# Attention on one core: the bank of a head's output sums changes place with a bank of the transposed scores at every new head

## The reference

```python
qkv = jnp.einsum('btd,de->bte', x, w_qkv) + b_qkv
q, k, v = heads(q), heads(k), heads(v)          # (4, 16, 2048, 16)
q, k = _rope(q), _rope(k)
attn = jnp.einsum('bhqd,bhkd->bhqk', q, k) / math.sqrt(HEAD_DIM)
attn = jax.nn.softmax(attn, axis=-1)
out = jnp.einsum('bhqk,bhkd->bhqd', attn, v)
x = _layernorm(x + out.reshape(b, t, d) @ w_out + b_out)      # shortened
x = _layernorm(x + (silu(x @ wg.T) * (x @ wu.T)) @ wd.T)      # shortened
```

## Time and profile before

| | |
|---|---|
| runs, device us | 2869.18, 2868.82, 2866.64 |
| span of the profiled execution | 2868.1 us |
| mean granted TensorE clock | 0.989 |
| PE matmul / DVE / ACT / POOL busy | 98% / 94% / 90% / 49% |
| copies of the sums (line 1032) | 64, the first at 274.6 us, the last at 2546.3 us |

### The profile page before, as it was taken

One profiled execution on the slowest core, in us unless ns is written; L12 is line 12 of the kernel. 1 busy time (PEld: TensorE's weight loads), 2 busy tenths in 40 slices (PEclk: granted clock), 3 DMA queues, 4 the chain that ended last, 5 costly groups with the idle time before them and its releaser, 6 DMA issues. The chain is left out here.

```text
span 2868.1 us, 70575 instructions
## 1 busy us (share of the span) xinstructions
PE 2811.7 (98%) x27022; PEld 862.5 (30%) x27022; DVE 2702.9 (94%) x3088; ACT 2591.9 (90%) x4778; POOL 1416.7 (49%) x4133
## 2 busy tenths in 40 slices
PE   8989999999999999999999999999999999999998
PEld 4531222222222222222222222222222222246665
DVE  7989999999999999999999999999999999947777
ACT  5756999999999999999999999999999999976555
POOL 7851444444444444444444444444444444436553
PEclk9978999999999999999999999999999999999999
DMA  5431111111111111111111111111111111233431
GB/s 194 142 116 28 36 35 36 35 36 35 35 35 35 34 35 36 35 36 36 35 35 35 36 35 35 35 35 36 35 35 36 35 35 35 70 90 92 118 96 38
DMA packets 121519, 146.56 MB, mean 51 GB/s; under 512 B 52832, under 2 KB 87520, under 8 KB 121180
## 3 DMA queue, kind: packets, MB, share of 16 engines
q1 hardware_dynamic: 120892, 142.02, 17.0%
q10 hardware_dynamic: 288, 0.01, 0.0%
HBM read 106.30 MB, written 35.13 MB: 49 GB/s over the span
## 5 line engine op out<-in xcount | busy, mean ns | idle before, releaser
L102 DVE TENSOR_REDUCE tile_max<-s_ps 128x1 f32<-128x1024 f32 (+1 forms) x2048 | 2282.4, 1185 | 8.8 <-PE s_ps L91 2.8
L1063 ACT ACTIVATE probs<-st_ps 128x512 f32<-128x512 f32 x4096 | 2202.2, 601 | 71.0 <-PE st_ps L942 41.1
L953 PE MATMUL o_ps<-probs,kept_v 128*17 128x256 f32 x16384 | 1283.1, 385 | 25.7 <-ACT sums L1032 25.7
L91 PE MATMUL s_ps<-k,q 64*128 64x512 f16 x4096 | 1266.2, 386 | 11.0 <-DVE tile_max L102 9.2
L942 PE MATMUL st_ps<-q,k 64*128 64x512 f16 x4096 | 1249.5, 382 | 1.1 <-ACT probs L1063 0.8
L1198 POOL TENSOR_TENSOR larger<-spared 128x256 f32<-128x256 f32 x1107 | 342.8, 310 | 675.6 <-ACT spared L1038 598.5
L953 PEld LDWEIGHTS o_ps<-probs,kept_v 128*17 128x17 f32 x16384 | 273.6, 95 | 852.2 <-ACT probs L1063 445.6
L942 PEld LDWEIGHTS st_ps<-q,k 64*128 64x128 f16 x4096 | 256.1, 94 | 902.0 <-ACT probs L1063 842.3
L1207 POOL TENSOR_TENSOR spared<-spared,larger 128x256 f32<-128x256 f32 x984 | 318.4, 324 | 81.9
L1200 POOL TENSOR_SCALAR larger<-larger 128x256 f32<-128x256 f32 x1107 | 261.4, 236 | 96.8
L91 PEld LDWEIGHTS s_ps<-k,q 64*128 64x128 f16 x4096 | 250.2, 94 | 50.4 <-DVE tile_max L102 46.5
(11 more groups left out here) (119 smaller groups left out, 1625.3 us busy)
## 6 DMA issues: line engine op xcount, KB each, us to landing
q<-q_parts SPq DMA_DIRECT2D x193, 128.0 KB
k<-k_parts SPq DMA_DIRECT2D x193, 128.0 KB
x_t<-in_x_t SPq DMA_DIRECT2D x16, 512.0 KB, 7.2
q_parts<-parts SPq DMA_DIRECT2D x32, 256.0 KB, 2.6
k_parts<-parts SPq DMA_DIRECT2D x32, 256.0 KB, 2.6
heads_out<-sums SPq DMA_DIRECT2D x256, 32.0 KB, 2.1
kept_v<-heads_out SPq DMA_DIRECT2D x16, 512.0 KB, 6.1
kept_v<-inverses_out SPq DMA_DIRECT2D x32, 256.0 KB
```

The source lines that it names most:

```text
L91: mm = pe.matmul(s["s_ps"][g % 2][:, j * BANK:(j + 1) * BANK], s["q"][h % 2][rows, r // KW * P:(r // KW + 1) * P], s["k"][h % 2][rows, at: ...
L102: dve.tensor_reduce(s["tile_max"][h % 2][:, r // KW, r % KW:r % KW + 1], s["s_ps"][g % 2][:, columns], AX.X, ALU.max).then_inc(s["s_read"], 1)
L953: mm = pe.matmul(o_ps[c * 32:c * 32 + VM, at:at + HALF], t["kept"][:, h, kt, :], probs[(h * KT + kt) % RING][:, c * BANK + at:c * BANK + a ...
L1063: act.activation(probs[(h * KT + kt) % RING][:, c * BANK:(c + 1) * BANK], st_ps[n % ST][:, :], ACT.Exp, scale=scale).then_inc(exp_done, 1)
```

## The change

There are four banks, `bank_ps0` to `bank_ps3`, and a table made before the program is written says which one each score and each head's sums use. Head 0 sums in bank 3, and its scores go round banks 0 to 2. The sums of every later head use the bank in which its own score 4 stood. That place in the ring would next be used by score 7 (4 + 3); score 7 and those after it in that place use the bank of the head before's sums instead.

The waits follow. The first sums of a head wait for one more exponential, that of score 4, and no longer for the copy of the head before. Score 7 waits for that copy, and no longer for the exponential of score 4 (which ScalarE does before the copy). Nothing else is added or taken away: the numbers of matmuls, exponentials and copies are the same.

```diff
+    HANDED = QC
+    ring = list(range(ST))
+    sum_bank, score_bank = [ST], []
+    for h in range(HEADS):
+        if h > 0:
+            sum_bank.append(ring[(h * EXPS + HANDED) % ST])
+        for e in range(EXPS):
+            if h > 0 and e == HANDED + ST:
+                ring[(h * EXPS + e) % ST] = sum_bank[h - 1]
+            score_bank.append(ring[(h * EXPS + e) % ST])
...
-        st_ps = [psum(f"st_ps{i}", [P, BANK]) for i in range(ST)]
-        o_ps = psum("o_ps", [P, BANK])
+        banks = [psum(f"bank_ps{i}", [P, BANK]) for i in range(ST + 1)]
+        st_ps = [banks[i] for i in score_bank]
+        o_ps = [banks[i] for i in sum_bank]
...
-                wait(pe, exp_done, n - ST + 1)
-                pe.matmul(st_ps[n % ST][:, :], k[h % 2][rows, kt * P:(kt + 1) * P],
+                if h > 0 and e == HANDED + ST:
+                    pe.wait_ge(sums_out, h)
+                else:
+                    wait(pe, exp_done, n - ST + 1)
+                pe.matmul(st_ps[n][:, :], k[h % 2][rows, kt * P:(kt + 1) * P],
                           q[h % 2][rows, c * BANK:(c + 1) * BANK], start=True, stop=True).then_inc(st_done, 1)
...
-                    pe.wait_ge(exp_done, h * EXPS + (kt + 1) * QC)
-                    if kt == 0:
-                        wait(pe, sums_out, h)
+                    handed = kt == 0 and h > 0
+                    pe.wait_ge(exp_done, h * EXPS + (HANDED + 1 if handed else (kt + 1) * QC))
...
-                    mm = pe.matmul(o_ps[c * 32:c * 32 + VM, at:at + HALF], t["kept"][:, h, kt, :],
+                    mm = pe.matmul(o_ps[h][c * 32:c * 32 + VM, at:at + HALF], t["kept"][:, h, kt, :],
...
-                act.copy(out["sums"][i][:, :], o_ps[:, :]).then_inc(sums_out, 1)
+                act.copy(out["sums"][i][:, :], o_ps[h][:, :]).then_inc(sums_out, 1)
```

More of the change, by code:

```diff
@@ L1062, in _ @@
                     act.wait_ge(st_done, n + 1)
-                    act.activation(probs[(h * KT + kt) % RING][:, c * BANK:(c + 1) * BANK], st_ps[n % ST][:, :],
+                    act.activation(probs[(h * KT + kt) % RING][:, c * BANK:(c + 1) * BANK], st_ps[n][:, :],
                                    ACT.Exp, scale=scale).then_inc(exp_done, 1)
-                    if e == QC and h > 0:
+                    if e == HANDED and h > 0:
                         drain(h - 1)
@@ L1077, in clear @@
             def clear():
-                dve.memset(o_ps[:, :], 0.0).then_inc(o_cleared, 1)
+                dve.memset(o_ps[0][:, :], 0.0).then_inc(o_cleared, 1)
                 for i in range(2):
```

## The result

The changed kernel takes 2852.91 us (median of 5 runs, 2850.06 to 2857.02), the kernel before 2868.82 (2866.64 to 2869.18): a ratio of 0.9948, 95% interval 0.9936 to 0.9960. The forecast was 2855.6 us, with a range of 2852 to 2862. The span of the profiled execution went from 2868.1 to 2851.1 us.

The account below looks back on a forecast made before the run. VectorE was taken to set the pace, except where TensorE's lead is used up. Handover 8.1 us, second halved tile 4.9 and last head 0.2 make 13.2 us: 2868.8 - 13.2 = 2855.6 us, 80% range 2852 to 2862.

Parts of the forecast that it names:

- What sets the pace: VectorE's reductions, 1.13 us from start to start, set a head's pace, except at three places where TensorE's lead is used up.
- The handover: Where a new head's sums waited for the copy: VectorE stops losing 0.13 us a head, 62 heads, 8.1 us.
- The new wait for the exponential of score 4: At a head's first sums: costs nothing, with no margin; TensorE comes by itself at 813.84, the wait ends at 813.83.
- The new wait of score 7: Score 7 waits for the copy of the sums: costs nothing, with 0.08 us of margin.
- the slower rival: Copy seen later at score 7 delays the next tile: 0.34 us lost a head against 0.13 now, 2882 us; chance 0.04.
- The halved tile behind the handover: Second halved tile, seven places behind the handover: VectorE's 2.09 us becomes 2.01, 0.08 us a head, 61 heads, 4.9 us.
- the model: The other halved tile of a head, taken to have TensorE's full lead: 2.01 us, the value expected at the second place.
- three places at which TensorE's lead is used up: The handover (the copy of the sums) and the two halved tiles; elsewhere VectorE sets the pace of a head.
- The last head: Head 63, where VectorE has no tiles: TensorE's 0.21 us wait for the copy counted whole as gain, 0.2 us.
- The sum: Handover 8.1 us, second halved tile 4.9 us and head 63 0.2 us: together 13.2 us, main case chance 0.62.
- VectorE's idle time by its busy share: Rival that VectorE is full already: only its idle 0.08 us a head can be won, 5.0 us, 2863.8; chance 0.08.
- TensorE's 25.7 us of waits, priced whole: Counting TensorE's 63 waits for the copy as the gain gives 25.7 us; by VectorE's starts about half of that.

Follow-up runs that it names:

- e6: Changed kernel with one halved tile a head in place of two, the one at place 10 being a full tile again: 2874.73 us, ratio 1.0025.
- e4: Changed kernel with the copy of the sums one exponential later on ScalarE's list, behind that of score 5: 2866.06 us, ratio 0.9995.
- e5: Changed kernel with the copy of the sums two exponentials later on ScalarE's list, behind that of score 6: 2897.52 us, ratio 1.0108.
- e1: Changed kernel with its rotating banks, but a head's first sums wait again for the copy of the head before: 2868.42 us, ratio 1.0002.
- e2: Kernel before the change, with the second halved tile and the reciprocal moved from place 10 to place 12: 2864.5 us, ratio 0.9987.
- e3: Changed kernel with the second halved tile and the reciprocal moved from place 10 to place 12: 2852.32 us, ratio 0.9944.
- e8: Changed kernel with both halves of each tile ahead of the even score on TensorE's list, nothing left out: 2844.67 us, ratio 0.9918.

## Why the prediction was right, step by step

- What sets the pace: VectorE, as forecast. e6 shows it directly, e4 and e5 by what TensorE's waits cost.
- The handover, 0.13 us a head, 8.1 us: right. Forecast were the sums 0.46 us before VectorE's next start (813.84 to 814.30), score 7 0.10 after it, the tile 0.14 after it, its second half 0.37 to 0.52 after it. Measured: -0.46 (774.16), 0.10 (774.72), 0.14 (774.76), 0.44 (775.06). The new wait for the exponential of score 4 cost nothing. e1 gives the whole gain back with the wait alone.
- The new wait of score 7: no cost, with the small margin that was forecast. e4 and e5 measure it: half a microsecond more and the gain is gone. This is the slower rival's mechanism; it is real, and it does not act at the place where the copy stands.
- The halved tile behind the handover: the effect was forecast, its size too small. This is the term that was mis-sized: 0.08 us a head, 4.9 us, was put at the nearest row's value with a bound of 0.09; measured are 0.13 us (2.096 to 1.966, medians of the 61 places), x 61 = 7.9 us. Two things were wrong in it. The bound took the gap of up to 0.26 us behind the reciprocal for VectorE's own time; part of it was a wait, and it is now 783.32 - 783.14 = 0.18, and 0.16 between full tiles in e6. And the halved tile that served as the model does not have quite the full lead in ScalarE's chain: the score behind the copy follows 1.51 us after the reduction at the first place now (784.05 - 782.54), 1.55 at the model (799.64 - 798.09). ScalarE's copy itself starts 0.36 us after the reduction at the first, 0.40 at the model:

```profile
782.90 0.59 ACT L1051 COPY spared<-s_ps 128x512 f32<-128x512 f32 x1
...
798.49 0.59 ACT L1051 COPY spared<-s_ps 128x512 f32<-128x512 f32 x1
```

  The model is the third tile of its head. The prediction named three places at which TensorE's lead is used up; it also shrinks at the first tile of a head, which stands two tiles ahead of the model. VectorE's start, and TensorE's start of that first tile (kernel after):

```profile
794.70 1.21 DVE L102 TENSOR_REDUCE tile_max<-s_ps 128x1 f32<-128x1024 f32 x1
...
794.92 0.37 PE L91 MATMUL s_ps<-k,q 64*128 64x512 f16 x1
```

  That is 0.23 us behind VectorE (full digits) in place of 0.14, in every head and in every run. It costs VectorE nothing by itself, but TensorE wins back only 0.04 us a tile, so at the model it has only just caught up. The halved tile before the model, fourteen places ahead of it, is not the reason: in e6 there is none for 32 places, and the model costs 2.01 us there too. What makes the first tile of a head late is not shown. A lead that is not quite whole shows in e2 as well: 2.02 us at nine places behind a stall, against 1.97 in e3 without one.
- The last head, 0.2 us: wrong in sign. There score 7 waits for the copy 0.39 us, where the sums waited 0.21: in the last head score 7 stands ahead of the sums on TensorE's list (2491.83 and 2492.15 in the trace after), so there the change asks for the copy earlier, not later. And from the last copy but one to the last it is 38.27 us in place of 38.04. It is too small to see in the time.
- The sum: 62 x 0.134 + 61 x 0.130 = 16.2 us, against 13.2 forecast, 17.0 between the spans and 15.9 between the medians. Of the 0.8 us that remain between the spans, 0.2 are the other halved tile (2.009 to 2.005 us, x 62), and the rest lies in single heads: one head of the trace before took 36.27 us for no reason that I can name, and the head before the last gained more (41.05 for 41.46).
- VectorE's idle time by its busy share, 0.08 us a head, was a rival. The head gained 0.27 us: where recorded lengths overlap, the share hides stalls. The Trainium skill (Perfetto Trace Analysis, Identifying the Most-Contended Engine) calls VectorE's occupancy a fair measure of how close it is to its limit; this case's traces do not agree. TensorE's 25.7 us of waits, priced whole, would have given 1.6 times the gain; the busy share, 5.0 us, gave a third of it.

## What to carry to other kernels

Find the engine that sets the pace by the distance between its starts, and price a wait on another engine by what it takes from the pacing one: here 25.7 us of TensorE's waits were worth 16 us, and 24.0 us of them in another place 13.5. A stall also costs at the next tight place downstream, because it uses up the lead that would have covered it; half of this gain lay seven places behind the edit. And a row that is to serve as a model for another has to be looked at for delays of its own: the model here stood two tiles behind one, which is a part of why that term came out too small. In a list that is worked in order, put the instruction that the pacing engine waits for ahead of one that may itself wait (e8: 8 us more, for swapping one pair of rows in every place).

## What the runs showed of the hardware that was not expected

A 128x1024 reduction on VectorE, 1.13 us from start to start and recorded 1.21 to 1.22 us long, took 1.08 us and was recorded 1.16 long when it stood behind a short reciprocal that itself stood behind a full tile (786.36 to 787.44 in e6, and so in 61 heads). Every trace has two such places outside the heads with halved tiles, one with the transpose and one with the reciprocal. In the kernel after:

```profile
226.43 0.20 DVE L1108 STREAM_TRANSPOSE top_t<-head_top 128x32 f32<-128x32 f32 x1
226.55 1.18 DVE L102 TENSOR_REDUCE tile_max<-s_ps 128x1 f32<-128x1024 f32 x1
...
2471.22 0.24 DVE L745 RECIPROCAL spread<-spread 128x16 f32<-128x16 f32 x1
2471.38 1.16 DVE L102 TENSOR_REDUCE tile_max<-s_ps 128x1 f32<-128x1024 f32 x1
```

Behind a halved tile the reduction after the same short operations was recorded 1.22 to 1.23 us long in all traces. So the short operation ahead does not shorten it by itself. Nor does a tile that is ready in time: at the handover of the kernel after it was, and the reductions there are recorded 1.21 us long. What makes the difference is not shown.
